# A vision tower's token stage: products read straight from the image tile, joined with the first normalization

## The chip, the cores and the metric

The kernel runs on one core of a Trainium2 chip. The metric is the device time of one execution in microseconds. A core has five engines that work side by side: TensorE (PE; its weight loads are PEld), VectorE (DVE), ScalarE (ACT), GpSimd (POOL) and SyncE (SP), which here only issues DMAs. They meet at semaphores. TensorE writes into eight PSUM banks of 128 partitions x 512 fp32.

## The reference

64 images of 3 x 224 x 224 become tokens, one attention block runs over them, then four experts and a head. The change touches the first two lines only:

```
patches = X.reshape(B, 3, 8, 28, 8, 28).transpose(0, 2, 4, 1, 3, 5).reshape(B, 64, 2352)
tokens  = einsum('bpi,hi->bph', patches, W) + b
tokens  = concat([class_token, tokens], axis=1) * pos_embed        # (64, 65, 128)
h = tokens + attention(layernorm(tokens))
h = h + experts(layernorm(h))
```

So each of the 64 patches of an image is a sum over 3 channels x 28 rows x 28 columns, and the normalization is over the 128 features of a token: subtract the mean, divide by the root of the variance + 1e-5. All of it is in fp32.

## The kernel before

Features lie in partitions and tokens in the free dimension: `h` and `z` are 128 x 4160 (64 images x 65 tokens). The stages follow each other in blocks; every engine finishes a block before the next is opened, and at each opening the semaphores of the stage before are cleared.

**Token stage** (`tokens_stage`, L201). A chunk is four images (`XI`), so there are 16. SP loads a chunk with 12 DMAs (L253), one for each channel and image, into `image[84, slot, 4, 8, 224]`: partition = channel x 28 + row within the patch, and in the free dimension image, patch row and the 224 pixels of a line. There are two slots. The sum over a patch's 28 columns is made as products that add up in PSUM. For one column the moving operand has 84 rows and 256 tokens, and these 256 elements lie 28 elements (112 bytes) apart in `image`. The kernel doesn't multiply them there. It first copies them side by side into `packed[128, slot, 21, 256]`: 21 columns by VectorE (L338), and the rows of the other 7 columns are spread over partitions 96 to 127 of the same 21 places, two parts by ScalarE (L306) and one by VectorE (L340). So 21 products of 128 rows (L292) do the work of 28. VectorE then stores the result with bias and positional factor into `h` (L345, `store`). The order on VectorE is written out: pack of a chunk, then store of the one before. SP loads a slot again when both packers are done with it (L260, L261); TensorE waits for both packers and for the store of two chunks before (L290).

Ahead of the loop the token weights are loaded as `w_rows[128, 84 x 28]`, turned by 28 transposes (L279), whose stationary operand takes 84 elements 28 apart, and copied to `w_cols` (L319, L322). The unused partitions are zeroed by memsets (L268, L311, L312).

**First normalization** (`norm_stage`, L362, called with the tag "n1_"). Ten steps of 416 tokens. For each: TensorE multiplies by `center` (L416, identity minus 1/128), ScalarE copies it out (L440) and squares it (L442), TensorE multiplies by `mean` (L422, 1/128 everywhere), ScalarE takes the root (L434), VectorE the reciprocal (L453), and GpSimd multiplies into `z` (L401). Buffers are double. The same function runs once more behind the attention ("n2_").

**First attention** (`first_attention_stage`) then reads `z`. `shared.ring` is a tile of 128 x 7680 fp32 that only later stages use.

Of the kernel before, what the change touches and what calls it, by code (L numbers as in the profile page):

```python
# [16 lines left out]
ALU = mybir.AluOpType  # L17
ACT = mybir.ActivationFunctionType
AX = mybir.AxisListType
ds = bass.ds  # L20

P = 128
# [175 lines left out]

def tokens_stage(nc, signals, ps, io, h0, ident, w_rows):  # L201

    XI = 4
    SLOTS = 2
    TRIPS = IMAGES // XI // SLOTS
    NP = GRID * GRID
    WHOLE = 21
    SPLIT = ((0, 32), (32, 64), (64, ROWS))
    HIGH = 96
    assert WHOLE == len(SPLIT) * (PATCH - WHOLE)  # L210
    with ExitStack() as ctx:
        sb = lambda name, shape: ctx.enter_context(nc.sbuf_tensor(name, shape, F32))
        sem = signals.stage()
        image = sb("image", [ROWS, SLOTS, XI, GRID, SIDE])
        packed = sb("packed", [P, SLOTS, WHOLE, XI * NP])
        w_cols = sb("w_cols", [P, WHOLE, P])
# [4 lines left out]
        clsp = sb("clsp", [P, 1])  # L221
        loaded = [sem(f"image_loaded{i}") for i in range(SLOTS)]
        consts, w_in = sem("consts_loaded"), sem("w_loaded")
        id_zero, id_done = sem("id_zeroed"), sem("id_done")
        turned, kept, padded = sem("w_turned"), sem("w_kept"), sem("rows_padded")
        packed_act, packed_dve = sem("packed_by_act"), sem("packed_by_dve")
        summed, stored, cls_done = sem("tok_summed"), sem("tok_stored"), sem("cls_done")
        block = open_block(nc, ctx, signals)
        turns = PATCH // 4

        def whole(s):

            return (packed[0:ROWS, s].rearrange("p q (r j) -> p q r j", j=GRID),
                    image[:, s].rearrange("p b g (j q) -> p q (b g) j", q=PATCH)[:, 0:WHOLE])

        def part(s, k):

            lo, hi = SPLIT[k]
            return (packed[HIGH:HIGH + hi - lo, s, k:WHOLE:len(SPLIT)].rearrange("p q (r j) -> p q r j", j=GRID),
                    image[lo:hi, s].rearrange("p b g (j q) -> p q (b g) j", q=PATCH)[:, WHOLE:PATCH])  # L240

        @block.sync
        def _(sp):
            sp.dma_start(w_rows[:, :], io["tok_W"]).then_inc(w_in, 16)
# [4 lines left out]
            def load(chunk, s):  # L249
                for c in range(CHANNELS):  # L250
                    for b in range(XI):
                        src = io["x"][ds(chunk * XI + b, 1), c].rearrange("a (g p) w -> p (a g) w", p=PATCH)
                        sp.dma_start(image[c * PATCH:(c + 1) * PATCH, s, b], src).then_inc(loaded[s], 16)  # L253

            for s in range(SLOTS):
                load(s, s)
            with sp.Fori(0, TRIPS - 1) as i:
                for s in range(SLOTS):

                    sp.wait_ge(packed_act, BASE + i * SLOTS + s + 1)  # L260
                    sp.wait_ge(packed_dve, BASE + i * SLOTS + s + 1)  # L261
                    load((i + 1) * SLOTS + s, s)

        @block.gpsimd
        def _(pool):
            make_identity(pool, ident, id_zero, id_done)
            pool.wait_ge(id_done, BASE + 1)
            pool.memset(packed[64:P, 1], 0.0).then_inc(padded, 1)  # L268

        @block.tensor  # L270
        def _(pe):
            pe.wait_ge(w_in, BASE + 16)
            pe.wait_ge(id_done, BASE + 1)
            w_view = w_rows[:, :].rearrange("p (r q) -> p r q", q=PATCH)
            for g in range(turns):
                if g >= 4:
                    pe.wait_ge(kept, BASE + g - 3)
# [7 lines left out]
            with pe.Fori(0, TRIPS) as i:  # L285
                for s in range(SLOTS):
                    pe.wait_ge(packed_act, BASE + i * SLOTS + s + 1)
                    pe.wait_ge(packed_dve, BASE + i * SLOTS + s + 1)

                    pe.wait_ge(stored, BASE + i * SLOTS + s - 1)  # L290
                    for q in range(WHOLE):
                        m = pe.matmul(ps[:, s, 0:XI * NP], w_cols[:, q, :], packed[:, s, q, :],  # L292
                                      start=(q == 0), stop=(q == WHOLE - 1))
                    m.then_inc(summed, 1)

        @block.scalar
        def _(act):
            act.wait_ge(padded, BASE + 3)
            with act.Fori(0, TRIPS) as i:
                for s in range(SLOTS):  # L300
                    act.wait_ge(loaded[s], BASE + (i + 1) * 16 * CHANNELS * XI)

                    act.wait_ge(summed, BASE + i * SLOTS + s - 1)
                    for k in range(2):
                        to, of = part(s, k)
                        op = act.copy(to, of)  # L306
                    op.then_inc(packed_act, 1)

        @block.vector
        def _(dve):  # L310
            dve.memset(packed[64:P, 0], 0.0).then_inc(padded, 1)  # L311
            dve.memset(w_cols[64:P], 0.0).then_inc(padded, 1)  # L312
            dve.wait_ge(padded, BASE + 3)
            for g in range(turns):
                dve.wait_ge(turned, BASE + g + 1)
                now = ps[0:ROWS, g % 4, :].rearrange("p (j m) -> p j m", j=4)
                here = min(max(WHOLE - 4 * g, 0), 4)
                if here:
                    op = dve.tensor_copy(w_cols[0:ROWS, 4 * g:4 * g + here, :], now[:, 0:here, :])  # L319
                for k, (lo, hi) in enumerate(SPLIT if here < 4 else ()):  # L320
                    at = len(SPLIT) * (4 * g + here - WHOLE) + k
                    op = dve.tensor_copy(w_cols[HIGH:HIGH + hi - lo, at:at + len(SPLIT) * (3 - here) + 1:len(SPLIT), :],  # L322
                                         now[lo:hi, here:4, :])
                op.then_inc(kept, 1)
# [8 lines left out]
            def pack(i, s):  # L333
                dve.wait_ge(loaded[s], BASE + (i + 1) * 16 * CHANNELS * XI)

                dve.wait_ge(summed, BASE + i * SLOTS + s - 1)
                to, of = whole(s)
                dve.tensor_copy(to, of)  # L338
                to, of = part(s, 2)
                dve.tensor_copy(to, of).then_inc(packed_dve, 1)  # L340

            def store(i, s):
                dve.wait_ge(summed, BASE + i * SLOTS + s + 1)
                out = h0[:, ds((i * SLOTS + s) * XI * SEQ, XI * SEQ)].rearrange("p (b s) -> p b s", s=SEQ)
                dve.scalar_tensor_tensor(  # L345
                    out=out[:, :, 1:SEQ], in0=ps[:, s, 0:XI * NP].rearrange("p (b t) -> p b t", t=NP),
                    scalar=bias[:, 0:1], in1=pos[:, 1:SEQ].unsqueeze(1).broadcast_to([P, XI, NP]),
                    op0=ALU.add, op1=ALU.mult).then_inc(stored, 1)

            pack(0, 0)  # L350
            pack(0, 1)
            store(0, 0)
            with dve.Fori(0, TRIPS - 1) as i:
                pack(i + 1, 0)
                store(i, 1)
                pack(i + 1, 1)
                store(i + 1, 0)
            store(TRIPS - 1, 1)

def norm_stage(nc, signals, ps, tag, src, dst, add, spill):  # L362
# [2317 lines left out]
```

## Time and profile before

| | us |
|---|---|
| median of 3 runs | 4192.47 (4190.81 to 4195.63) |
| profiled execution, own time | 4191.02 |
| its span in the trace | 4189.3 |
| TensorE busy over the span | 3695.9 (88%) |
| VectorE busy | 2841.8 (68%) |
| ScalarE busy | 2150.3 (51%) |
| GpSimd busy | 1278.5 (31%) |

The profile is one execution. Matmuls overlap in it (their ends are modelled), so what matters of them is how far apart they start. An fp32 product shows as two records. "Idle before" is the time in which an engine did nothing ahead of a group, with what ended it.

### The profile page before, as it was taken

Reading aid. Unit: us, or ns where it says so; the run is one execution under the profiler, and the core shown is the slowest. Engines: PE = TensorE matmul, PEld = TensorE weight load, DVE = VectorE, ACT = ScalarE, POOL = GpSimd, SP = SyncE. Lnnn points to the kernel's source line nnn. Section 1 sums busy time; section 2 is a strip of 40 time slices with the busy share of each in tenths; the row PEclk is TensorE's granted clock in tenths of the full one; section 3 lists DMA queues with packets and bytes.
Section 4 is the critical chain, followed back from the end, with each engine's and each line's share of the span. In section 5 each row is a group of like instructions: output and inputs, shape, how many; then the busy total and the mean of one; then the engine's idle time right before and its main releaser. Section 6 shows DMA issues by size and latency. Waiting matters only on the chain. (4 is left out here: it accounts for less than half of the span.)

```text
span 4189.3 us, 98294 instructions
## 1 busy us (share of the span) xinstructions
PE 3695.9 (88%) x36068; PEld 2265.2 (54%) x36068; DVE 2841.8 (68%) x5015; ACT 2150.3 (51%) x4378; POOL 1278.5 (31%) x1076
## 2 busy tenths in 40 slices
PE   5869689979988998952999999999999959999998
PEld 4645346646655655631555555555555527666665
DVE  8966568858858857876666666666666664555555
ACT  4536437737746755755444444444444445555554
POOL 0027537627726736744000000000000003444443
PEclk8889899989999999975999999999999978999999
DMA  8910100010010011025111111111111131111111
GB/s 174 176 33 0 52 18 2 1 56 2 0 42 16 0 42 32 0 87 157 46 50 48 45 48 50 48 44 48 49 49 43 49 103 52 54 53 53 53 53 30
DMA packets 392895, 205.07 MB, mean 49 GB/s; under 512 B 151221, under 2 KB 386474, under 8 KB 392106
## 3 DMA queue, kind: packets, MB, share of 16 engines
q1 hardware_dynamic: 392354, 203.09, 18.9%
q8 instruction: 88, 1.44, 0.1%
q14 instruction: 61, 0.50, 0.0%
q10 hardware_dynamic: 392, 0.03, 0.0%
HBM read 145.55 MB, written 57.51 MB: 48 GB/s over the span
## 5 line engine op out<-in xcount | busy, mean ns | idle before, releaser
L1827 PE MATMUL banks<-l_w,l_xs 128*64 128x512 f16 x6240 | 722.3, 381 | 15.0 <-DVE l_xs L1875 14.2
L1827 PE MATMUL banks<-l_w,l_hs 128*64 128x512 f16 x6144 | 705.8, 379 | 1.7 <-DVE l_hs L1881 1.7
L1827 PEld LDWEIGHTS banks<-l_w,l_xs 128*64 128x64 f16 x6240 | 344.6, 110 | 330.7 <-issue 25.6
L1827 PEld LDWEIGHTS banks<-l_w,l_hs 128*64 128x64 f16 x6144 | 348.3, 110 | 316.7 <-DVE l_hs L1881 2.2
L194 POOL MEMSET h_ident<- 128x128 f32 x1 | 0.2, 204 | 1444.3 <-POOLq L81 1444.3
L985 POOL TENSOR_TENSOR ax_p<-ax_p,ax_ri 128x520 f32<-128x520 f32 (+1 forms) x256 | 320.0, 1251 | 267.4 <-DVE ax_ri L1185 267.4
L1932 DVE SCALAR_TENSOR_TENSOR l_gates<-banks,l_unscale,l_bias 128x1024 f32<-128x1024 f32 x260 | 333.8, 1284 | 96.1 <-PE banks L1827 94.7
L1988 ACT ACTIVATE l_gates<-l_gates 128x768 f32<-128x768 f32 x260 | 219.1, 843 | 347.4 <-DVE l_gates L1932 347.4
L2259 PE MATMUL banks<-h_mem,h_w 128*128 128x320 f16 x2496 | 357.9, 300 | 1.0 <-DMA h_mem<-mem_scratch 1.0
L2554 ACT ACTIVATE h_work<-banks,h_bias,h_factor 128x320 f32<-128x320 f32 x312 | 192.3, 616 | 262.8 <-PE banks L2259 259.1
L2259 PEld LDWEIGHTS banks<-h_mem,h_w 128*128 128x128 f16 x2496 | 244.4, 98 | 94.9 <-issue 1.6
L956 POOL TENSOR_TENSOR ax_km<-ax_k,ax_mask 128x512 f32<-128x512 f32 x256 | 290.6, 1136 | 6.0 <-PE banks L1067 6.0
L1992 ACT ACTIVATE l_ig<-l_cell 128x256 f32<-128x256 f32 x260 | 108.3, 416 | 358.2 <-DVE l_cell L1949 356.2
L1263 ACT ACTIVATE ax_p<-ax_p 128x520 f32<-128x520 f32 (+1 forms) x256 | 170.5, 666 | 202.7 <-DVE ax_p L1177 202.0
L999 PE MATMUL banks<-ax_x,w_in 128*128 128x256 f16 (+1 forms) x1632 | 198.3, 274 | 81.3 <-DVE ax_x L1149 54.1
L1945 DVE TENSOR_TENSOR l_ig<-l_gates 128x256 f32<-128x256 f32 x256 | 109.0, 426 | 210.0 <-ACT l_gates L1989 210.0
L1172 DVE TENSOR_REDUCE ax_mx<-banks 128x8 f32<-128x520 f32 (+1 forms) x256 | 186.0, 727 | 84.0 <-PE banks L1067 83.8
L292 PE MATMUL banks<-packed,w_cols 128*128 128x256 f32 x672 | 174.8, 427 | 56.8 <-DVE packed L340 56.8
L999 PEld LDWEIGHTS banks<-ax_x,w_in 128*128 128x128 f16 x1632 | 146.6, 100 | 122.4 <-DVE ax_x L1149 68.8
L1177 DVE TENSOR_TENSOR ax_p<-banks,ax_mx 128x520 f32<-128x520 f32 (+1 forms) x256 | 187.9, 734 | 31.2 <-DVE ax_mx L1172 13.9
L1953 DVE TENSOR_TENSOR l_hid<-l_gates,l_ig 128x256 f32<-128x256 f32 x260 | 110.8, 426 | 130.1 <-ACT l_ig L1992 130.1
L292 PEld LDWEIGHTS banks<-packed,w_cols 128*128 128x128 f32 x672 | 144.4, 217 | 86.9 <-issue 62.9
(306 smaller groups left out, 7180.4 us busy)
## 6 DMA issues: line engine op xcount, KB each, us to landing
image<-in_x_dram SPq DMA_DIRECT2D x192, 196.0 KB
l_x<-x_scratch SPq DMA_DIRECT2D x130, 256.0 KB, 3.0
mem_scratch<-l_hs SPq DMA_DIRECT2D x520, 64.0 KB, 1.9
h_mem<-mem_scratch SPq DMA_DIRECT2D x104, 320.0 KB, 3.7
x_scratch<-x_out SPq DMA_DIRECT2D x4, 4160.0 KB, 16.4
raw_in<-in_L_ffn_attn_in_w_dram SPq DMA_DIRECT2D x4, 768.0 KB, 4.5
h_scratch<-x_out SPq DMA_DIRECT2D x1, 2080.0 KB, 6.5
z_scratch<-z SPq DMA_DIRECT2D x1, 2080.0 KB, 11.6
```

Of the source, the lines that this page charges most:

```text
L292: m = pe.matmul(ps[:, s, 0:XI * NP], w_cols[:, q, :], packed[:, s, q, :], start=(q == 0), stop=(q == WHOLE - 1))
L956: pool.tensor_tensor(self.km[:, s % 2], self.k[:, par, :, s, :].unsqueeze(2).broadcast_to([P, KD, 4, self.KEYS]), self.mask4[:, :].unsquee ...
L985: pool.tensor_tensor(self.p[:, v, :, 0:k], self.p[:, v, :, 0:k], self.ri[:, v, :, 0:k].unsqueeze(3).broadcast_to([P, 2, k, SEQ]), ALU.mult ...
L999: mm = pe.matmul(bank, w_in[:, k, b, at:at + P], x[:, a, k], start=(k == 0 and i == 0), stop=(k == KD - 1 and i == len(PASSES) - 1))
L1172: dve.tensor_reduce(self.mx[:, s % 2, :, 0:k], now, AX.X, ALU.max).then_inc(self.maxed, 1)
L1177: dve.tensor_tensor(self.p[:, v, :, 0:k], now, self.mx[:, s % 2, :, 0:k].unsqueeze(3).broadcast_to([P, 2, k, SEQ]), ALU.subtract).then_inc ...
L1263: act.activation(self.p[:, s % 4, :, 0:k], self.p[:, s % 4, :, 0:k], ACT.Exp, scale=SCALE).then_inc(self.exped, 1)
L1827: mm = pe.matmul(ps[d * HALF:(d + 1) * HALF, 2 * z + n, :], lhsT, w_of[e][:, d, kk, b, n * 512:(n + 1) * 512], start=(kk == 0 and turn_ == ...
L1932: dve.scalar_tensor_tensor(out=gz.rearrange("p (n c) -> p n c", n=2), in0=ps[:, 2 * z:2 * z + 2, :], scalar=unscale[:, e:e + 1], in1=bias[ ...
L1988: act.activation(gates[:, z, 0:3 * D], gates[:, z, 0:3 * D], ACT.Sigmoid).then_inc(gated, 1)
L2259: mm = pe.matmul(ps[:, bank, 0:W], w[:, e, b, here:here + P], moving(k, a), start=(k == 0 and turn_ == 0), stop=(k == nk - 1 and turn_ == 2))
L2554: act.activation(dst[:, m, :], ps[:, bank, 0:W], func, bias=bias(m), scale=factor[:, e, at:at + 1]).then_inc(S[name + "_kept"], 1)
```

## The change

The token stage and the first normalization become one stage. Nothing is copied: the moving operand of each product is the image tile itself, 84 rows and 256 elements 112 bytes apart (`column`), so there are 28 products for a chunk instead of 21. The packing, its tiles and the memsets are gone. There are four image slots; the fourth lies in `shared.ring`. SP loads a slot again when its products are done (`summed`). The loops of the stage are written out. The normalization goes in steps of one chunk (260 tokens), with its products behind those of the next chunks on TensorE and its reciprocals behind the stores on VectorE. The second normalization is as before.

```
 # SP
+            for n in range(CHUNKS):
+                s = n % SLOTS
+                if n >= SLOTS:
+                    sp.wait_ge(summed, BASE + n - SLOTS + 1)
                 for c in range(CHANNELS):
                     for b in range(XI):
+                        src = io["x"][n * XI + b, c].rearrange("(g p) w -> p g w", p=PATCH)
+                        sp.dma_start(image[s][c * PATCH:(c + 1) * PATCH, b], src).then_inc(loaded[s], 16)
 # GpSimd
+            for n in range(CHUNKS):
+                pool.wait_ge(inverted, BASE + n + 1)
+                pool.tensor_tensor(span(z, n), xc[:, n % 2, :], rs[:, n % 2, :], ALU.mult).then_inc(normed, 1)
 # TensorE
+            for n in range(CHUNKS + 2):
+                if n < CHUNKS:
+                    pe.wait_ge(loaded[n % SLOTS], BASE + (n // SLOTS + 1) * 16 * CHANNELS * XI)
+                    if n >= 2:
+                        pe.wait_ge(stored, BASE + n - 1)
+                    for q in range(PATCH):
+                        m = pe.matmul(ps[:, n % 2, 0:XI * NP], w_cols[:, q, :], column(n % SLOTS, q),
+                                      start=(q == 0), stop=(q == PATCH - 1))
                     m.then_inc(summed, 1)
+                if 1 <= n <= CHUNKS:
+                    pe.wait_ge(stored, BASE + n)
+                    if n >= 3:
+                        pe.wait_ge(copied, BASE + n - 2)
+                    pe.matmul(ps[:, 2 + (n - 1) % 2, 0:SPAN], center[:, :], span(h0, n - 1), start=True,
+                              stop=True).then_inc(centered, 1)
+                if n >= 2:
+                    pe.wait_ge(squared, BASE + n - 1)
+                    if n >= 4:
+                        pe.wait_ge(rooted, BASE + n - 3)
+                    pe.matmul(ps[:, 4 + n % 2, 0:SPAN], mean[:, :], sq[:, n % 2, :], start=True, stop=True).then_inc(varied, 1)
 # ScalarE
+            for n in range(CHUNKS + 3):
+                if 2 <= n < CHUNKS + 2:
+                    m = n - 2
+                    act.wait_ge(centered, BASE + m + 1)
+                    if m >= 2:
+                        act.wait_ge(normed, BASE + m - 1)
+                    act.copy(xc[:, m % 2, :], ps[:, 2 + m % 2, 0:SPAN]).then_inc(copied, 1)
...
+                    act.activation(sq[:, m % 2, :], xc[:, m % 2, :], ACT.Square).then_inc(squared, 1)
+                if n >= 3:
+                    m = n - 3
+                    act.wait_ge(varied, BASE + m + 1)
...
+                    act.activation(sd[:, m % 2, :], ps[:, 4 + m % 2, 0:SPAN], ACT.Sqrt, bias=eps[:, 0:1]).then_inc(rooted, 1)
 # VectorE
+            for n in range(CHUNKS + 4):
+                if 1 <= n <= CHUNKS:
+                    m = n - 1
+                    dve.wait_ge(summed, BASE + m + 1)
+                    dve.scalar_tensor_tensor(
...
+                if n >= 4:
+                    m = n - 4
+                    dve.wait_ge(rooted, BASE + m + 1)
+                    if m >= 2:
+                        dve.wait_ge(normed, BASE + m - 1)
+                    dve.reciprocal(rs[:, m % 2, :], sd[:, m % 2, :]).then_inc(inverted, 1)
 # front
-        tokens_stage(nc, signals, ps, io, h, ident, z[:, 0:ROWS * PATCH])
+        tokens_stage(nc, signals, shared, ps, io, h, z, ident)
         attended = sb("attended", [P, TOKENS])
-        norm_stage(nc, signals, ps, "n1_", h, z, None, None)
```

## Rows read from the trace of the kernel before

**Rows 1.** The page: span, and the DMA engines' busy share in 40 slices.
```profile
span 4189.3 us, 98294 instructions
DMA  8910100010010011025111111111111131111111
```

**Rows 2.** Stretches: start:end us, length, each engine busy (records), clock, DMA share, GB/s.
```profile
35.30:228.40 193.10, 153.13 (x590) 126.52 (x589) 175.25 (x42) 106.74 (x36) 0.00 (x0) 0.87 0.92 175
228.40:250.55 22.15, 20.63 (x83) 17.06 (x81) 13.01 (x4) 6.94 (x2) 0.00 (x0) 0.88 0.00 0
250.55:292.60 42.05, 19.18 (x40) 7.40 (x40) 27.53 (x11) 17.79 (x31) 11.28 (x14) 0.87 0.00 0
```

**Rows 3.** Groups by line and form, 0 to 450 us: busy us, mean ns | idle before.
```profile
L292 PE MATMUL banks<-packed,w_cols 128*128 128x256 f32 x672 | 174.8, 427 | 56.8 <-DVE packed L340 56.8
L338 DVE COPY packed<-image 84x5376 f32<-84x5376 f32 x16 | 160.5, 10034 | 21.4 <-DMA image<-in_x_dram 21.4
L306 ACT COPY packed<-image 32x1792 f32<-32x1792 f32 x32 | 111.6, 3486 | 42.2 <-DMA image<-in_x_dram 42.0
L340 DVE COPY packed<-image 20x1792 f32<-20x1792 f32 x16 | 31.9, 1995 | 0.2
```

**Rows 4.** Timeline at the end of the token stage: start us, length us, instruction.
```profile
227.33 12.37 PE L292 MATMUL banks<-packed,w_cols 128*128 128x256 f32 x42 [3.17 <-DVE packed L340]
...
228.41 10.03 DVE L338 COPY packed<-image 84x5376 f32<-84x5376 f32 x1 [0.81 <-DMA image<-in_x_dram]
...
240.70 9.33 PE L292 MATMUL banks<-packed,w_cols 128*128 128x256 f32 x42 [1.00 <-DVE packed L340]
250.07 0.48 DVE L345 SCALAR_TENSOR_TENSOR x_out<-banks,tok_bias,pos 128x256 f32<-128x256 f32 x1 [9.09 <-PE banks L292]
```

**Rows 5.** Timeline of the first two chunks.
```profile
22.13 9.93 DVE L338 COPY packed<-image 84x5376 f32<-84x5376 f32 x1 [2.94 <-DMA image<-in_x_dram]
...
34.31 11.61 PE L292 MATMUL banks<-packed,w_cols 128*128 128x256 f32 x42 [15.83 <-DVE packed L340]
35.27 10.04 DVE L338 COPY packed<-image 84x5376 f32<-84x5376 f32 x1 [1.21 <-DMA image<-in_x_dram]
```

**Rows 6.** Stretches early in the token stage.
```profile
20.00:30.00 10.00, 0.00 (x0) 0.00 (x0) 7.87 (x1) 7.78 (x3) 0.00 (x0) 0.50 1.00 180
...
40.00:60.00 20.00, 15.24 (x70) 12.78 (x68) 17.98 (x5) 10.60 (x4) 0.00 (x0) 0.99 0.98 181
```

**Rows 7.** First normalization: two groups, then the timeline at its end.
```profile
L453 DVE RECIPROCAL n_rs<-n_sd 128x416 f32<-128x416 f32 x10 | 27.5, 2752 | 13.3 <-ACT n_sd L434 11.8 <-POOL z L401 1.4
...
L442 ACT ACTIVATE n_sq<-n_xc 128x416 f32<-128x416 f32 x10 | 5.5, 549 | 0.3
...
291.49 1.06 POOL L401 TENSOR_TENSOR z<-n_xc,n_rs 128x416 f32<-128x416 f32 x1 [2.64 <-DVE n_rs L453]
294.18 0.42 SPq L1293 DMA_DIRECT2D a_rows<-in_L_attn_w_qkv_dram  x1
```

**Rows 8.** Groups of 260 columns in the attention stage.
```profile
L602 PE MATMUL banks<-a_x,a_cols 128*128 128x260 f32 x64 | 19.2, 425 | 1.0 <-DVE a_cols L1314 1.0
L784 ACT COPY a_k<-banks 128x260 f32<-128x260 f32 x16 | 6.0, 376 | 1.0 <-PE banks L602 0.4
L571 POOL TENSOR_TENSOR a_p<-a_p,a_ri 128x260 f32<-128x260 f32 x48 | 30.7, 640 | 29.0 <-DVE a_ri L739 29.0
```

**Rows 9.** Strided and contiguous fp32 reads; weight loads (min/median/max or mean ns).
```profile
L2612 ACT COPY h_z2s<-h_h 128x4160 f32<-128x4160 f32 x1 | 7.6, 7640 | 0.0
L1988 ACT ACTIVATE l_gates<-l_gates 128x768 f32<-128x768 f32 x260 | 219.1, 843 | 347.4 <-DVE l_gates L1932 347.4
L279 PEld LDWEIGHTS banks<-ident,z x7: 152/154/178, 12.4 to 13.2; 128*84 128x84 f32 x7
L691 PEld LDWEIGHTS banks<-ident,a_p x256: 133/137/138, 309.4 to 461.7; 128*65 128x65 f32 x128
L699 PEld LDWEIGHTS banks<-a_pt,a_v 65*32 65x32 f32 x896 | 15.3, 109 | 9.6 <-issue 9.6
```

More of the change, by code:

```diff
@@ L213, in tokens_stage @@
         sem = signals.stage()
-        image = sb("image", [ROWS, SLOTS, XI, GRID, SIDE])
-        packed = sb("packed", [P, SLOTS, WHOLE, XI * NP])
-        w_cols = sb("w_cols", [P, WHOLE, P])
+        w_rows = z[:, 0:ROWS * PATCH]
+        own = sb("image", [ROWS, SLOTS - 1, XI, GRID, SIDE])
+        image = [own[:, s] for s in range(SLOTS - 1)]
+        image.append(shared.ring[0:ROWS, 0:XI * GRID * SIDE].rearrange("p (b g w) -> p b g w", b=XI, g=GRID))
+        w_cols = sb("w_cols", [ROWS, PATCH, P])
         pos_rows = sb("pos_rows", [SEQ, P])
@@ L221, in tokens_stage, with column @@
         clsp = sb("clsp", [P, 1])
+        center = sb("n1_center", [P, P])
+        mean = sb("n1_mean", [P, P])
+        eps = sb("n1_eps", [P, 1])
+        xc = sb("n1_xc", [P, 2, SPAN])
+        sq = sb("n1_sq", [P, 2, SPAN])
+        sd = sb("n1_sd", [P, 2, SPAN])
+        rs = sb("n1_rs", [P, 2, SPAN])
         loaded = [sem(f"image_loaded{i}") for i in range(SLOTS)]
         consts, w_in = sem("consts_loaded"), sem("w_loaded")
-        id_zero, id_done = sem("id_zeroed"), sem("id_done")
-        turned, kept, padded = sem("w_turned"), sem("w_kept"), sem("rows_padded")
-        packed_act, packed_dve = sem("packed_by_act"), sem("packed_by_dve")
+        id_zero, id_done, zero, ready = sem("id_zeroed"), sem("id_done"), sem("n1_zero"), sem("n1_ready")
+        turned, kept = sem("w_turned"), sem("w_kept")
         summed, stored, cls_done = sem("tok_summed"), sem("tok_stored"), sem("cls_done")
+        centered, copied, squared, varied, rooted, inverted, normed = [
+            sem("n1_" + n) for n in ("centered", "copied", "squared", "varied", "rooted", "inverted", "normed")]
         block = open_block(nc, ctx, signals)
         turns = PATCH // 4
[L231 to L240, printed above, removed]
+        def column(s, q):
+            return image[s].rearrange("p b g (j q) -> p q (b g) j", q=PATCH)[:, q]
+        span = lambda a, n: a[:, n * SPAN:(n + 1) * SPAN]
         @block.sync
         def _(sp):
-            sp.dma_start(w_rows[:, :], io["tok_W"]).then_inc(w_in, 16)
+            sp.dma_start(w_rows, io["tok_W"]).then_inc(w_in, 16)
             sp.dma_start(pos_rows[:, :], io["pos"]).then_inc(consts, 16)
@@ L247, in _ @@
             sp.dma_start(cls[:, :], io["cls"].rearrange("a p -> p a")).then_inc(consts, 16)
-            def load(chunk, s):
+            for n in range(CHUNKS):
+                s = n % SLOTS
+                if n >= SLOTS:
+                    sp.wait_ge(summed, BASE + n - SLOTS + 1)
                 for c in range(CHANNELS):
                     for b in range(XI):
[L252 to L262, printed above, removed]
+                        src = io["x"][n * XI + b, c].rearrange("(g p) w -> p g w", p=PATCH)
+                        sp.dma_start(image[s][c * PATCH:(c + 1) * PATCH, b], src).then_inc(loaded[s], 16)
         @block.gpsimd
@@ L284, in _ @@
             pe.wait_ge(kept, BASE + turns + 1)
[L285 to L293, printed above, removed]
-                    m.then_inc(summed, 1)
+            pe.wait_ge(ready, BASE + 3)
@@ L296, in _ @@
         @block.scalar
         def _(act):
[L298 to L307, printed above, removed]
+            act.wait_ge(ready, BASE + 3)
@@ L309, in _ @@
         @block.vector
         def _(dve):
-            dve.memset(packed[64:P, 0], 0.0).then_inc(padded, 1)
-            dve.memset(w_cols[64:P], 0.0).then_inc(padded, 1)
-            dve.wait_ge(padded, BASE + 3)
             for g in range(turns):
                 dve.wait_ge(turned, BASE + g + 1)
[L316 to L324, printed above, removed]
+                dve.tensor_copy(w_cols[:, 4 * g:4 * g + 4, :],
+                                ps[0:ROWS, g % 4, :].rearrange("p (j m) -> p j m", j=4)).then_inc(kept, 1)
@@ L331, in _ @@
             dve.tensor_copy(h0_view[:, :, 0], clsp[:, :].broadcast_to([P, IMAGES])).then_inc(cls_done, 1)
[L333 to L358, printed above, removed]
+            dve.wait_ge(cls_done, BASE + 2)
+            for n in range(CHUNKS + 4):
[3 more added lines that the diff above has]
+                    dve.scalar_tensor_tensor(
+                        out=h0_view[:, m * XI:(m + 1) * XI, 1:SEQ],
+                        in0=ps[:, m % 2, 0:XI * NP].rearrange("p (b t) -> p b t", t=NP), scalar=bias[:, 0:1],
+                        in1=pos[:, 1:SEQ].unsqueeze(1).broadcast_to([P, XI, NP]), op0=ALU.add, op1=ALU.mult).then_inc(stored, 1)
+                if n >= 4:
+                    m = n - 4
+                    dve.wait_ge(rooted, BASE + m + 1)
+                    if m >= 2:
+                        dve.wait_ge(normed, BASE + m - 1)
+                    dve.reciprocal(rs[:, m % 2, :], sd[:, m % 2, :]).then_inc(inverted, 1)
 def norm_stage(nc, signals, ps, tag, src, dst, add, spill):
```

25 lines of the change are left out of this document (16 added, 9 removed).

## The prediction

> **What bounds the kernel now.** The page shows a span of 4189.3 us and, in its slices, the DMA engines near full only in the first 6% [rows 1]. That is the stage the change rewrites, so I cut the start of the trace into stretches [rows 2]. Until 228.4 us the image streams in with a DMA share of 0.92 while VectorE is busy 175 of 193 us and TensorE 153; from there to 250.55 the last chunk is packed and multiplied with no DMA at all; from 250.55 to 292.6 the first normalization runs alone, every engine below two thirds busy. Everything behind 292.6 is unchanged text, so the change is worth what it takes off these 292.6 us.
>
> In the token stage a chunk of four images costs VectorE 10.03 + 1.99 us of packing plus 0.48 for the store, and ScalarE two copies of 3.49 [rows 3, 4]. A slot is loaded again only when it is packed, so load and packing alternate on two slots: chunk 0 is there at 22.1 us, chunk 15 at 228.4, 13.75 us a chunk. With a full queue the loads take less: chunk 1 landed 13.1 us after chunk 0 [rows 5], and the fullest windows move 180 to 181 GB/s [rows 6], which is 13.35 us for the 2.408 MB of a chunk. So DMA is the floor of this stage, and the packing adds 0.4 us a chunk and 12 us at the end, where chunk 15 is packed with nothing beside it.
>
> **Part 1: packing goes.** 12.0 us of VectorE and 7.0 of ScalarE a chunk disappear. Beside the DMA they hid, apart from the 0.4 us a chunk (6 us over 15 chunks) and 12.3 us between landing (228.4) and first product (240.7) of the last chunk [rows 4].
>
> **Part 2: products, 28 for 21.** The last run of 42 records (two to a product) took 9.33 us at full clock, 0.218 us a record after the first [rows 4]. 56 records are 12.2 us. The first run after an idle stretch costs more: 11.61 us where the stretch before had a granted clock of 0.50, the lower level (1.2 GHz), and 12.37 for a later one with gaps [rows 5, 4], so 2.3 to 3.0 us once, at the start. Then TensorE also gets the two normalization products of 260 columns, four records of 0.222 us, 0.9 us a chunk (the 260-column rows of the attention stage have the same length as the 256-column ones, within the per-column step [rows 8]). Sum: 13.1 us a chunk against 13.35 for DMA. The two are almost level, so TensorE has gaps of a few tenths of a microsecond, where now they are 1 to 5 us, and I expect it to stay at full clock.
>
> The moving operand is what no row shows: 256 fp32 elements 112 bytes apart instead of side by side. Bounds come from the nearest rows of strided fp32 reads [rows 9, 3]. ScalarE read 4160 elements 260 bytes apart in 7.64 us, 1.84 ns each, while its contiguous 768 took 0.843 us, 1.1 ns with the fixed part: about a doubling. VectorE's 20-partition copy reads this very image with this very step at 1.11 ns. TensorE's own weight loads read the token weights with this same 112-byte step: 84 columns in 154 ns, where 32 and 65 contiguous columns took 109 and 137 ns, 0.85 ns a column; that line gives 153 ns for 84. No stall is left to put down to the step. I take this row, because it is the same engine and fp32 too, and a moving record of 0.218 us is 0.85 ns a column, the same pace. So the term is 12.2 us; the ends kept for the range are 0.85 and 1.84 ns a column.
>
> The Trainium skill speaks against it. "SBUF — State Buffer", Specifications (TRN2), gives 16-byte cachelines that need at least two hits per line for full bandwidth. With one fp32 element per line that would double each record, and the sum would be the slow rival's below; ScalarE's row agrees with it, the weight loads' does not.
>
> **Part 3: loads run free.** Four slots, and a slot is given back by the products instead of the packing. The load of chunk n waits for the products of n-4, which end three chunk times before the queue needs it, so SP never lets the queue run dry. The weights go ahead of chunk 0 as now, so chunk 0 is ready at 22.1. Chunk 15 lands at 22.1 + 15 x 13.35 = 222.3. TensorE alone would begin it at 22.1 + 2.6 + 15 x 13.1 = 221.2. The later one decides: products end at 222.3 + 12.2 + about 0.5 for waits = 235.0. The loops that are now written out add instruction fetches; no row before shows TensorE on long written-out text beside full queues, so I take nothing for them, as the loads of chunk n are covered by the products of the chunks before, and keep 1 us a chunk as the upper end (16 us, the high end of the forecast's own range).
>
> **Part 4: normalization moves beside the products.** Removed: all 42.0 us of the stage [rows 2]. Added per chunk, scaled from 416 to 260 columns or read at 260: reciprocal 2.75 x 260/416 = 1.72 us on VectorE, multiply 0.64 on GpSimd, copy 0.38, square about 0.4 and root about 0.45 on ScalarE [rows 7, 8]. VectorE then does 0.5 + 1.7 us in 13.35, ScalarE 1.2, GpSimd 0.64: all hidden under DMA. The added waits on TensorE stand in its queue ahead of the next products: "stored" of the chunk before, "copied" and "squared" of the one before that. All three are signalled at the latest 5 us after the products before, thus 8 us early.
>
> What doesn't hide is the tail, because the order is laid out with a lag. On VectorE the reciprocal of chunk n-4 stands behind the store of n-1, so when the last products end, four reciprocals (12 to 15) are still to come, and the copy of a chunk waits for the multiply of the one two before it. Followed through, from the products' end: store 0.5, reciprocal 12 to 2.2, multiply 3.0, copy and square of 14 to 3.9, root 13 to 4.3, reciprocal 13 to 6.1, multiply 6.8, copy and square of 15 to 7.7, root 14 to 8.2, reciprocal 14 to 9.9, reciprocal 15 to 11.7, multiply to 12.4. The stage ends at 235.0 + 12.4 = 247.4, where now the last multiply ends at 292.55 [rows 7]: 45.1 us less. One opening of a block between stages goes with it and is inside those 42 us; the attention's opening clears 22 semaphores instead of 10, for which I give back 0.3 us. Its first transfer follows now 1.6 us behind the last multiply [rows 7], and will again.
>
> **Sum.** 4191.02 (the profiled execution; 1.7 outside its span) - 44.8 = 4146.2. The median of the runs is 1.45 above the profiled one, so 4147.7 us.
>
> **Rivals.**
> Slow rival, slower than before: the moving read pays for the step as ScalarE does. A doubled record is 0.436 us, a chunk 24.4 + 0.9 = 25.3 us, TensorE becomes the bound: 22.1 + 16 x 25.3 + 11.5 = 438.4, 145.9 us later than 292.5, time 4338. At ScalarE's 1.84 ns (0.471 us a record) it is 4371. It decides from the point where TensorE's chunk is (292.5 - 22.1 - 11.5)/16 = 16.2 us, thus 0.273 us a record, 1.07 ns a column. For it: ScalarE's row, and the 84-partition copy at 10.03 us for 5376 elements, 1.87 ns. Against it: the weight loads, and the 20-partition copy. Half-way stands VectorE's 1.11 ns: 0.284 us a record, 16.8 us a chunk, 302 us, time 4202.
> Second rival, a smaller gain: TensorE falls to the lower clock between chunks, as it does now in gaps of 2 to 5 us (mean clock 0.87 [rows 2]). 2 us more a chunk make TensorE the bound at 15.1 us: 22.1 + 241.6 + 11.5 = 275, time 4175. Against it: the gaps become short.
> Third, that the change gains only its packing half: if a wait chain held the normalization behind the products, TensorE would stall 3 to 4 us a chunk for it, 16.5 us a chunk, no gain: 4195. The program order above gives each signal a chunk of time, so little speaks for this.
>
> **How the numbers follow.** Forecast 0.66, with a range of its own of 4140 to 4160 (the low end has DMA at 13.1 us a chunk, the high end 1 us more a chunk on TensorE). Smaller gain 0.07, half-way 0.06, slow rival 0.18, third 0.03. What a measurement can tell from no change is 0.2%, 8.4 us. Faster: forecast and second rival, 0.72 with a share of the half-way case below its centre. Same: 0.04. Slower: 0.24. To leave out no more than 2 in 10 the range must reach the doubled record: 4139 to 4340.
>
> **What would show it.** A record of the products at 378 to 382 ns and 56 of them in about 12.4 us: part 2 right; records twice as far apart and a DMA share near 0.5: the slow rival. DMA share at 0.98 or more until 222 us: part 3. TensorE's granted clock at 1.00 from 40 us on: no second rival. Last multiply some 12 us behind the last product, with four reciprocals between: part 4. The attention's first transfer at about 249.3 us. The forecast is wrong if TensorE's chunk exceeds 14 us.

## The result and the profile after: slower by 4.4%

The changed kernel takes 4375.51 us (median of 4 runs, 4371.53 to 4377.8), the kernel before 4191.67 beside it (4 runs, 4190.81 to 4195.63). The ratio is 1.0436, 95% interval 1.0418 to 1.0454. The forecast of 4147.7 is wrong, and so is its range of 4139 to 4340; what came is the slow rival at ScalarE's price, 4371. The profiled execution took 4376.95 us.

The page after, against [rows 1]: its span, and 40 slices with the granted clock (tenths of full) and the DMA share.

```profile
span 4375.2 us, 98154 instructions
...
PEclk5555798999999999997699999999999997999999
DMA  7442001001001001002511111111111123121111
```

The loads, which filled the first 6% of the span before, now spread over four slices at falling shares, and the clock stands at its lower level (0.50, 1.2 GHz) for as long. The stretches of the stage, against [rows 2]:

```profile
22.10:50.00 27.90, 27.54 (x59) 18.55 (x60) 0.48 (x1) 0.00 (x0) 0.00 (x0) 0.50 1.00 184
50.00:200.00 150.00, 150.00 (x324) 98.76 (x323) 7.47 (x8) 8.11 (x16) 2.20 (x3) 0.53 0.57 109
200.00:430.00 230.00, 230.00 (x497) 150.43 (x496) 17.35 (x16) 9.28 (x24) 5.88 (x8) 0.54 0.33 63
```

TensorE is busy 150 us of 150 and 230 of 230 while DMA falls to 0.57 and 0.33 and VectorE does 7.5 us of work in 150: TensorE alone sets the pace. The groups, against [rows 3] (the packing lines are gone; L297 are the products, L360 the normalization's reciprocals, L273 its multiplies):

```profile
L297 PE MATMUL banks<-image,w_cols 84*128 84x256 f32 x672 | 315.7, 647 | 8.3 <-DMA image<-in_x_dram 8.3
...
L360 DVE RECIPROCAL n_rs<-n_sd 128x260 f32<-128x260 f32 x16 | 28.2, 1767 | 4.3 <-ACT n_sd L331 4.2
...
L273 POOL TENSOR_TENSOR z<-n_xc,n_rs 128x260 f32<-128x260 f32 x16 | 11.7, 734 | 460.4 <-DVE n_rs L360 460.4
```

647 ns is a record's duration; its pace is read from how far apart records start. The weight loads, one to a record, in a stretch where the clock was full, and the clock of two windows, one in it and one behind it:

```profile
161.10 0.21 PEld L297 LDWEIGHTS banks<-image,w_cols 84*128 84x128 f32 x1 [0.19 <-issue]
161.56 0.21 PEld L297 LDWEIGHTS banks<-image,w_cols 84*128 84x128 f32 x1 [0.26 <-issue]
162.03 0.21 PEld L297 LDWEIGHTS banks<-image,w_cols 84*128 84x128 f32 x1 [0.26 <-issue]
162.50 0.21 PEld L297 LDWEIGHTS banks<-image,w_cols 84*128 84x128 f32 x1 [0.26 <-issue]
```

```profile
161.00:162.00 1.00, 1.00 (x3) 0.42 (x2) 0.00 (x0) 0.96 (x3) 0.00 (x0) 1.00 0.95 178
...
170.00:174.00 4.00, 4.00 (x10) 2.76 (x9) 0.00 (x0) 0.00 (x0) 0.00 (x0) 0.50 0.34 61
```

They start 0.467 us apart at a granted clock of 1.00, and the ones from 170.43 on, at 0.50, stand 0.467 apart too (170.43, 170.90, 171.36). So the clock does not set the pace. That the read does is what the first experiment shows; by it an element costs 0.467/256 = 1.82 ns. 56 records take 26.1 us where 12.2 were forecast. With 0.9 to 1.7 us of normalization a chunk is 27.6 us: products run from 22.46 to 463.8.

The end of the stage, where the forecast had put four reciprocals:

```profile
464.29 1.78 DVE L360 RECIPROCAL n_rs<-n_sd 128x260 f32<-128x260 f32 x1
...
468.19 1.78 DVE L360 RECIPROCAL n_rs<-n_sd 128x260 f32<-128x260 f32 x1 [2.12 <-ACT n_sd L331]
...
472.09 3.42 DVE L360 RECIPROCAL n_rs<-n_sd 128x260 f32<-128x260 f32 x2 [2.12 <-ACT n_sd L331]
...
475.59 0.73 POOL L273 TENSOR_TENSOR z<-n_xc,n_rs 128x260 f32<-128x260 f32 x1 [0.91 <-DVE n_rs L360]
478.18 0.41 SPq L1294 DMA_DIRECT2D a_rows<-in_L_attn_w_qkv_dram  x1
```

The last multiply ends at 476.32, where before it ended at 292.55 [rows 7]: 183.8 us later. The profiled executions are 185.9 us apart, the medians 183.8.

### The profile page after: what moved, and what is told of

Its sections match the earlier page's. It is cut to its first block and busy times, and to the rows that moved or that the text cites. A ratio compares the mean times of both kernels' runs of the same rounds, so it can differ in the third digit from the quotient of the medians.

```text
span 4375.2 us, 98154 instructions
## 1 busy us (share of the span) xinstructions
PE 3951.9 (90%) x36316; PEld 2407.2 (55%) x36316; DVE 2636.4 (60%) x4982; ACT 2031.9 (46%) x4357; POOL 1275.0 (29%) x1081
## 5 line engine op out<-in xcount | busy, mean ns | idle before, releaser
L297 PE MATMUL banks<-image,w_cols 84*128 84x256 f32 x672 | 315.7, 647 | 8.3 <-DMA image<-in_x_dram 8.3
L297 PEld LDWEIGHTS banks<-image,w_cols 84*128 84x128 f32 x672 | 204.2, 304 | 116.3 <-issue 113.2
L1173 DVE TENSOR_REDUCE ax_mx<-banks 128x8 f32<-128x520 f32 (+1 forms) x256 | 185.9, 726 | 88.3 <-PE banks L1068 88.0
L1178 DVE TENSOR_TENSOR ax_p<-banks,ax_mx 128x520 f32<-128x520 f32 (+1 forms) x256 | 187.9, 734 | 29.8 <-DVE ax_mx L1173 12.4
```

The costliest lines, as they stand in the source:

```text
L297: m = pe.matmul(ps[:, n % 2, 0:XI * NP], w_cols[:, q, :], column(n % SLOTS, q), start=(q == 0), stop=(q == PATCH - 1))
L1173: dve.tensor_reduce(self.mx[:, s % 2, :, 0:k], now, AX.X, ALU.max).then_inc(self.maxed, 1)
L1178: dve.tensor_tensor(self.p[:, v, :, 0:k], now, self.mx[:, s % 2, :, 0:k].unsqueeze(3).broadcast_to([P, 2, k, SEQ]), ALU.subtract).then_inc ...
```

## Experiments

A run that was timed in rounds has an interval; the others are one profiled execution with its time. Line numbers differ a little between the kernels. Unless said otherwise the edit is made in the changed kernel.

### Moving elements side by side

Each product reads 256 neighbouring elements of the image tile, so the output isn't the tokens; all else is equal.

```
-            return image[s].rearrange("p b g (j q) -> p q (b g) j", q=PATCH)[:, q]
+            flat = image[s].rearrange("p b g w -> p (b g w)")
+            at = q // 1 * 1 * XI * NP + q % 1
+            return flat[:, at:at + 1 * (XI * NP - 1) + 1:1]
```

> The changed kernel, but the 256 elements of each product's moving operand lie side by side in the image tile instead of 112 bytes apart (the tile is read as if it were packed, so the tokens are not the reference's). Same 28 products, same 84 rows, same waits. Theory A (TensorE's moving read pays for the step; the low granted clock follows from it): records 0.218 us apart instead of 0.467, granted clock near 1.00, DMA share near 1 until about 222 us, time about 4148. Rival B (the low clock is the cause, because of 84 rows or of written-out text, and the step costs little): records 0.43 us apart at a granted clock of 0.50, time about 4340. If both count, records stay above 0.25 us and the time lands between 4180 and 4330.

4175.22 us (5 runs), ratio to before 0.9962 (0.9948 to 0.9976). 200 us come back, so the step is the cause. The timeline shows that 28 more are missing:

```profile
71.20 24.10 PE L299 MATMUL banks<-image,w_cols 84*128 84x256 f32 x56
95.09 1.07 PE L306 MATMUL banks<-x_out,n_center 128*128 128x260 f32 x2
95.96 0.71 PE L312 MATMUL banks<-n_sq,n_mean 128*128 128x260 f32 x2
96.51 12.25 PE L299 MATMUL banks<-ring,w_cols 84*128 84x256 f32 x56
```

```profile
22.50:95.00 72.50, 72.50 (x170) 57.33 (x171) 0.97 (x2) 2.08 (x3) 0.00 (x0) 0.50 0.89 162
...
98.00:200.00 102.00, 102.00 (x473) 89.64 (x472) 15.61 (x16) 8.95 (x23) 5.14 (x7) 1.00 0.99 175
```

Three chunks run at the lower clock, 24.1 us each, though TensorE is busy 72.5 us of 72.5. The clock rises only behind the first four records in a row of 128 rows, the two normalization products from 95.09 on; then a chunk takes 12.25, as forecast. The expectation of about 4148 had not seen these three chunks.

### Steps of 8 and of 16 bytes

The same with every second and every fourth element (`flat[:, at:at + 511:2]`, `flat[:, at:at + 1021:4]`).

> As the side-by-side kernel, but the moving elements lie 8 bytes apart (two fp32 in each 16 bytes). Theory A with 16-byte lines, as the Trainium skill's page SBUF — State Buffer, Specifications (TRN2), has them: two reads fall into a line, so full pace, records 0.218 us apart and about 4148. Rival A2 (any step beyond the next element costs the same): records 0.467 us apart and about 4375. Between them, a cost that grows with the step: about 0.24 us.

> As the side-by-side kernel, but the moving elements lie 16 bytes apart (one fp32 in each 16 bytes). Theory A with 16-byte lines: every read opens a new line, so records 0.467 us apart as at 112 bytes and about 4375. If the line is longer than 16 bytes (32 or 64): 0.218 us and about 4148.

4183.11 and 4364.26 us (4148 and 4375 expected; the 8-byte kernel too has three chunks of 24.1 us at the lower clock). First a chunk with 8 bytes at a granted clock of 1.00, then one with 16 at 0.50:

```profile
110.47 12.86 PE L299 MATMUL banks<-image,w_cols 84*128 84x256 f32 x56
```

```profile
128.31 25.57 PE L299 MATMUL banks<-image,w_cols 84*128 84x256 f32 x56
```

A record (the chunk less the last record's own 0.388 or 0.632 us, over 55) takes 0.2268 and 0.4534 us. 256 elements 8 bytes apart touch 128 pieces of 16 bytes, 16 bytes apart 256: 1.77 ns a piece in both. The 16-byte kernel also had a stretch at 1.00: its weight loads start at 183.21, 183.66, 184.11 and 184.56 us, 0.45 apart, so this price does not follow the clock. Side by side the elements touch 64 pieces, which would be 0.113 us and hides under the 0.2155 us that 256 columns take anyway at full clock. There a record takes the longer of columns x 0.84 ns and pieces x 1.77 ns; at 112 bytes a piece is 1.82. At the lower clock the columns take twice as long, 0.43 us a record, which hides 8 bytes altogether (24.1 us a chunk with it and without it) and 16 bytes nearly.

### bfloat16 halves, same step

```
+            flat = image[s].rearrange("p b g w -> p (b g w)").bitcast(BF16)
+            return flat[:, 2 * q + 1:2 * q + 1 + 2 * PATCH * (XI * NP - 1) + 1:2 * PATCH]
```

The products take the upper halves of weights and pixels as bf16 numbers: one record to a product instead of two, the same 256 places.

> The changed kernel, with each product on the upper halves of the fp32 values read as bf16, so with one record instead of two, the moving elements still 112 bytes apart (tokens only bf16-exact). Theory A1 (each address costs TensorE's moving read about 1.7 to 1.8 ns, whatever the type and the number of passes over it): 256 addresses, 0.43 to 0.47 us a record, 28 records a chunk = 12.0 to 13.1 us, so DMA bounds and the time is about 4150 to 4160. Rival A3 (an fp32 record reads its elements twice, so an address costs half of that): 0.22 to 0.24 us a record, 6.5 us a chunk. Both leave the time near 4145 to 4160; the distance of the records decides.

```profile
79.19 13.24 PE L299 MATMUL banks<-image,w_cols 84*128 84x256 bf16 x28
```

4162.85 us. 28 records in 13.24 us, less the last one's 0.647, are 0.466 us each, the fp32 record's pace. So neither the bytes of an element nor its type count, only how many places are read. Half the records halve the bill, and the granted clock stayed at 0.50 (22.5 to 200 us) beside a DMA share of 1.00.

### Weights strided, moving operand side by side

Beside the edit of the first experiment the stationary operand takes every 28th element of `w_cols`.

> The side-by-side kernel, but now the stationary operand is read with the step: its 128 fp32 elements lie 112 bytes apart in w_cols (tokens not the reference's). Theory G (weight loads do not pay for the step, as the token weights' turning in the kernel before seemed to show: 84 columns in 154 ns): records 0.2155 us apart at full clock, time as the side-by-side kernel's, about 4175. Rival H (the weight read pays as the moving read does, and what hid it in the kernel before is that a transpose's load is shorter than the spacing of its records): 128 addresses at 1.7 to 1.8 ns are 0.22 us a load or, if an fp32 load reads twice, 0.44 us, records 0.45 us apart, time about 4360.

```profile
124.63 12.88 PE L300 MATMUL banks<-image,w_cols 84*128 84x256 f32 x56
```

4181.32 us; 0.227 us a record against 0.2155. 128 places at 1.77 ns are 0.227: the weight load sets the pace and pays the same price. Side by side such a load takes 0.112 us at full clock (next section), so the step doubles it as well. It barely shows, because the product's 256 columns take 0.2155 anyway.

### The weight loads by themselves

Four groups of 28 instructions ahead of chunk 0, back to back.

```
+ pe.transpose(ps[0:ROWS, 7, 0:P], w_view[:, :, k], ident[:, :])
+ pe.transpose(ps[0:ROWS, 7, 0:P], w_rows[:, 84 * k:84 * k + 84], ident[:, :])
+ pe.matmul(ps[0:ROWS, 7, 0:32], w_view[:, :, k], ident[:, 0:32], start=True, stop=True)
+ pe.matmul(ps[0:ROWS, 7, 0:32], w_rows[:, 84 * k:84 * k + 84], ident[:, 0:32], start=True, stop=True)
```

> The changed kernel with four extra groups of 28 instructions on TensorE ahead of chunk 0, each back to back: transposes whose stationary operand is 84 columns of the token weights 112 bytes apart (as the kernel's own are), the same with the 84 columns side by side, and then fp32 products of 32 moving columns with the same two stationary operands, where the load is longer than the product and sets the pace. What is open is why the prediction's row (84 strided columns in 154 ns) showed no price for the step. Theory 1: the duration in that row is no measure of the read (154 ns is also 84 times 1.83 ns), and the strided load costs 1.77 ns an address as the moving operand does; then the strided product loads stand about 150 ns apart for a load, and the ones side by side clearly closer. Theory 2: a fp32 load is so slow by itself that the step hides under it (the 128 column load of the kernel with strided weights stood at 0.227 us against 0.213); then the two groups of products stand within 10% of each other and the row could not have shown the step whatever its price. The transposes, whose pace the 128 moving columns set (0.16 us apart in the kernel before), should be alike by either. The whole time is of no interest: 4376 plus about 2 us.

The groups in this order, strided, side by side, strided, side by side:

```profile
14.12 3.07 PEld L288 LDWEIGHTS banks<-ident,z 128*84 128x84 f32 x28 [1.49 <-DVE w_cols L345]
17.14 3.07 PEld L290 LDWEIGHTS banks<-ident,z 128*84 128x84 f32 x28
20.20 8.51 PEld L292 LDWEIGHTS banks<-ident,z 128*84 128x84 f32 x56
28.61 7.94 PEld L294 LDWEIGHTS banks<-ident,z 128*84 128x84 f32 x56
```

The transposes stand 0.11 us apart either way. Of the product loads, two to a product, the strided ones stand 0.150 apart and those side by side 0.140, within the 10% of theory 2. But the two groups didn't run at one clock. The stretches, and two groups of the changed kernel's own trace, further on, whose products have a single moving column and 128 weight columns side by side:

```profile
20.40:24.80 4.40, 4.40 (x32) 4.40 (x31) 0.00 (x0) 0.00 (x0) 0.00 (x0) 1.00 1.01 188
28.70:36.20 7.50, 7.50 (x55) 7.50 (x56) 0.00 (x0) 0.00 (x0) 0.00 (x0) 0.50 0.99 187
```

```profile
707.83 5.26 PE L1463 MATMUL banks<-x_vec,raw_in 128*128 128x1 f32 x24
1707.40 2.26 PE L1463 MATMUL banks<-x_vec,raw_in 128*128 128x1 f32 x19
```

The clock fell at 25.0 us, within the strided group, and its loads stand 0.150 apart before and behind: 84 places at 1.77 ns are 0.149. The group side by side had 0.50 throughout. The two lines of the changed kernel give 0.213 us a load at 0.50 and 0.112 at 1.00, thus 1.67 and 0.87 ns a column. At 0.50 that makes 0.140 for 84 columns, what the group took; at 1.00 it would be 0.073 (an estimate, by columns), and the strided load takes twice that. So theory 1 holds: the load of a product pays for the step, and the lower clock hid it here. The forecast's row [rows 9] was one of transposes, whose loads show no price at all. Why they go at 0.110 us with the step, below 84 x 1.77 = 0.149, stays open. The whole took 4391.19 us, 13 more than expected: the groups lie ahead of chunk 0, whose products began at 37.17 instead of 22.46, and TensorE had nothing to spare.

### Side by side, with the clock kept up

The first experiment, and 20 products over 128 rows (40 records of 256 columns) while chunk 0 is still in flight. In the first experiment the clock was at 1.00 from 10.8 us on, behind the transposes of the weights, and fell at 17.7, as TensorE waited for the first image; here it stays at 1.00 from 12.2 us on. So the extra products hold the clock rather than lift it.

```
+            for k in range(20):
+                at = k % 9 * XI * NP
+                pe.matmul(ps[:, 7, 0:XI * NP], center[:, :], z[:, at:at + XI * NP], start=True, stop=True)
```

> The side-by-side kernel (tokens not the reference's) with 20 products of 128 rows x 256 columns put on TensorE ahead of chunk 0, where it waits for the first image; their result is not used. Theory E (what kept the side-by-side kernel at the 1.2 GHz level for its first three chunks, 24.1 us each instead of 12.25, is that products of 84 rows do not raise the granted clock, but keep it once it is up; the 128-row products of the normalization raised it at 96 us): the clock is 1.00 from the first chunk, products at 0.2155 us a record throughout, last products end at about 235 us, time about 4148. Rival F (something of the stage's first 70 us, such as DMA traffic or the written-out text's first pass, holds the clock down): three slow chunks again, time about 4175.

```profile
36.00:200.00 164.00, 160.20 (x727) 137.13 (x728) 23.14 (x23) 15.10 (x34) 7.04 (x10) 1.00 1.00 180
```

4146.95 us (4 runs, 4143.44 to 4148.8), ratio 0.989 (0.9873 to 0.9906). That is the forecast's 4147.7: with the step and the low clock gone, DMA is full at 1.00, chunks take 12.25 to 12.35 us and the last products end at 236.4 (235.0 forecast). The clock is worth 4175.22 - 4146.95 = 28 us.

### The changed kernel, with the clock kept up

The same 20 products ahead of the changed kernel's own reads.

> The changed kernel as it is, with 20 products over 128 rows ahead of chunk 0 and nothing else. Theory: the address step of the moving operand sets 0.467 us a record at either clock, and a granted clock that is lifted first falls again within some us though TensorE stays busy; the time is about 4375 (4372 to 4380). Rival: the low granted clock is a cause of the slow records, and once lifted stays up as in the side-by-side kernel; then the chunks take less than 26 us and the time lies anywhere from 4150 to 4340.

```profile
23.00:26.00 3.00, 3.00 (x9) 1.54 (x8) 0.00 (x0) 0.00 (x0) 0.00 (x0) 1.00 0.99 176
26.00:28.00 2.00, 2.00 (x5) 0.83 (x4) 0.00 (x0) 0.00 (x0) 0.00 (x0) 1.00 1.01 176
28.00:30.00 2.00, 2.00 (x6) 1.33 (x5) 0.00 (x0) 0.00 (x0) 0.00 (x0) 0.53 0.99 177
30.00:34.00 4.00, 4.00 (x10) 2.68 (x9) 0.00 (x0) 0.00 (x0) 0.00 (x0) 0.50 0.99 184
```

4374.67 us, no gain. The clock stood at 1.00 at the start of the products and fell within 5 us with TensorE busy throughout. The low clock follows from the slow reads and is not their cause.

### Packing on VectorE alone

From the changed kernel: two image and two packed slots, and VectorE copies all 28 columns side by side; ScalarE copies nothing in the packing. The 28 products and the joined normalization stay.

```
+ dve.tensor_copy(packed[n % 2].rearrange("p q (r j) -> p q r j", j=GRID),
+                 image[n % SLOTS].rearrange("p b g (j q) -> p q (b g) j", q=PATCH)).then_inc(packed_dve, 1)
```

> All of the reference. One stage with the normalization, as in the changed kernel, but VectorE copies each chunk side by side (one copy of 84 x 7168, all 28 columns, nothing on ScalarE), two image slots and two packed slots, 28 products from the packed tile. Theory C (VectorE was slowed to 1.87 ns an element in the kernel before only by ScalarE reading the same partitions; alone it takes the 1.08 ns of its 20-partition copy): the copy takes 7.8 us, VectorE is busy 10.1 us a chunk, DMA stays the bound, the stage ends at about 222.3 + 7.8 + 12.2 + 13 = 255 us and the time is about 4154. Rival D (84 partitions at this step cost 1.87 ns whatever ScalarE does): 13.4 us a copy, VectorE 15.7 us a chunk, the stage ends at about 298 us, time about 4197.

```profile
L353 DVE COPY packed<-image 84x7168 f32<-84x7168 f32 x8 | 54.9, 6858 | 15.8 <-DMA image<-in_x_dram 15.8
...
L274 POOL TENSOR_TENSOR z<-n_xc,n_rs 128x260 f32<-128x260 f32 x16 | 44.1, 2754 | 238.3 <-DVE n_rs L367 238.3
```

4184.24 us (10 runs), ratio 0.9989 (0.9977 to 1.0001): no change that can be told. But the copy reads the same image with the same step at 6858/7168 = 0.96 ns an element, where before, beside ScalarE's packing, it took 10034/5376 = 1.87 [rows 3]. VectorE's packing fell from 12.0 to 6.9 us a chunk, though it now copies all columns. That ScalarE's reads had slowed it is the likely cause and not shown: no run has the old copy without ScalarE. The run again lost three chunks to the lower clock.

The 2754 ns of GpSimd's multiply are a mean of two cases, five of 7.1 to 7.2 us and eleven of 0.73. One of each:

```profile
119.16 6.77 DVE L353 COPY ring<-image 84x7168 f32<-84x7168 f32 x1
119.40 7.14 POOL L274 TENSOR_TENSOR z<-n_xc,n_rs 128x260 f32<-128x260 f32 x1 [115.21 <-DVE n_rs L367]
...
184.16 0.73 POOL L274 TENSOR_TENSOR z<-n_xc,n_rs 128x260 f32<-128x260 f32 x1 [5.75 <-DVE n_rs L367]
184.34 7.29 DVE L353 COPY packed<-image 84x7168 f32<-84x7168 f32 x1 [0.26 <-DMA image<-in_x_dram]
```

A multiply that begins behind VectorE's copy ends 0.6 us after it; where the multiply came first, the copy took 7.29 us instead of 6.77. The second of the two waits for the first.

### Packing on VectorE, with the clock up, three ways

First with 36 extra products as above.

> All of the reference. The kernel that packs with VectorE alone, with 36 products of 128 rows ahead of chunk 0 whose result is not used. Theory E: clock 1.00 from the first chunk, chunk 0's products begin at about 29.5 us, 13.0 us a chunk on TensorE against 13.35 to 14.1 us for the loads on two slots, last copy ends at about 229 to 238 us, last products at 242 to 251, stage end at 254 to 263 us: time 4153 to 4162. Rival F: as without the extra products, 4184.

4154.65 us (4 runs), ratio 0.9902 (0.9885 to 0.9918). Then without extra products: the packed tile and the weights get 128 rows, 84 to 127 zero, and each of the 28 products takes all 128.

```
-        beside = sb("packed", [ROWS, PATCH, XI * NP])
+        beside = sb("packed", [P, PATCH, XI * NP])
-        w_cols = sb("w_cols", [ROWS, PATCH, P])
+        w_cols = sb("w_cols", [P, PATCH, P])
```

> The kernel that packs on VectorE alone, but its 28 products a chunk take 128 rows of the packed tile (rows 84 to 127 hold zeros) in place of 84, and nothing else warms TensorE. First theory: what lifts the granted clock is how many rows a product takes, whatever their content. Then the clock is at 1.00 within a few us of the first product, there are no chunks of 24.1 us, and the time is about 4156 (4184.2 less two and a third slow chunks' excess of 12 us each). Rival: rows of zeros lift nothing; then the first three chunks take 24.1 us again and the time is about 4184.

```profile
33.81 14.23 PE L299 MATMUL banks<-packed,w_cols 128*128 128x256 f32 x56 [7.63 <-DVE packed L358]
47.88 12.25 PE L299 MATMUL banks<-ring,w_cols 128*128 128x256 f32 x56
```

4154.21 us (4 runs), ratio 0.991 (0.9895 to 0.9925). One chunk takes 2 us more, and no chunk 24.1: its records stand 0.43 us apart until 37.4 us, 3.5 us after the first, and 0.216 from 37.7 on. With 128 rows the pace of the full clock comes though 44 of them are zeros. At last the copy in two halves, a shorter normalization chain and 28 extra products.

```
+                        if q % HALF == 0:
+                            pe.wait_ge(packed_dve, BASE + 2 * n + 1 + q // HALF)
-            for n in range(CHUNKS + 4):
+            for n in range(CHUNKS + 3):
```

> The packing kernel with 28 warming products, the copy of a chunk in two halves of columns so that the products wait for a half only, and a shorter chain in the normalization (the reciprocal runs three tiles behind and not four, the root stands ahead of the copy and the square on ScalarE). If the tail and the wait for the first copy are on the path, as the traces of the changed kernel (12.6 us from last product to the end) and of the packing kernel show, 3.4 us go for the half copy and about 3.7 in the tail: about 4147.5 against 4154.65 for the warmed packing kernel. Rival: transfers set the pace of the middle chunks (DMA share 1.00 there), and what is gained at the start is waited for later; then only the tail's gain stays, about 4151.

```profile
186.22 0.60 PE L316 MATMUL banks<-n_sq,n_mean 128*128 128x260 f32 x2
189.00 23.94 PE L303 MATMUL banks<-packed,w_cols 84*128 84x256 f32 x56 [2.18 <-DVE packed L360]
...
214.46 13.32 PE L303 MATMUL banks<-ring,w_cols 84*128 84x256 f32 x56
```

4148.36 us (5 runs, 4139.97 to 4160.17), ratio 0.9893 (0.9878 to 0.9909). The median stands where expected (4147.5), but the interval doesn't part it from the two others. The profiled execution, 4160.17, shows one source of its spread: behind a wait of 2.18 us for a copy the clock fell, and the 84-row products ran a whole chunk at half pace; it rose again behind the next four records of 128 rows. That lost 12 us. All three take about 1% less than the kernel before.

## Why the prediction was wrong

**What bounds the kernel, and DMA as the floor** held: 4146.95 us with a DMA share of 1.00 once nothing else was slow.

**Part 2 failed, at the moving operand.** The step took its price from the weight loads, "No stall is left to put down to the step. I take this row, because it is the same engine and fp32 too". Measured: 1.82 ns a column, not 0.85, 0.467 us a record, 26.1 us a chunk, and TensorE became the bound. Two things were wrong with the row. They were loads of transposes, which show no price for the step (0.110 us apart with it and without it); the same columns loaded for a product cost 0.150, twice what side by side would. And durations were compared, three of them put on a line, where the pace of a row of records was needed. The ends kept for the read's price (0.85 and 1.84 ns) did hold the truth; the choice between them was the error. The full price was worked out as 4371 and left outside the range of 4139 to 4340, which reached only the doubled record at 4338. The stage ended 5.9 us later than the rival had it: 27.57 us a chunk instead of 27.3 (4.3 in 16), a tail of 12.6 instead of 11.5, and a start 0.4 later.

The rule of "SBUF — State Buffer", Specifications (TRN2) in the Trainium skill, at least two hits in each 16-byte line for full bandwidth, was told and given too little weight. The runs agree with it in the main: at full clock two hits a line cost 5%, one hit doubles the record.

**Part 2 also mis-sized the start.** "2.3 to 3.0 us once, at the start" came from products of 128 rows [rows 5]. With 84 rows the clock did not rise in 72.5 us; that cost 28 us in the side-by-side kernel. Without the step the change as written takes 4175, by chance the second rival's time, whose mechanism (gaps between chunks) it is not.

**Part 3** could not show in the changed kernel, where TensorE was late. In the side-by-side kernel with the clock up it was right to 1.4 us, and so was taking nothing for the written-out loops: the chunks there take 12.25 to 12.35 us.

**Part 4 was right.** From last product to last multiply 12.6 us (12.4 forecast), with four reciprocals of 1.77 us (1.72) and the chain in the order followed through. The attention's first transfer came 1.86 us behind it (1.6).

**Slow rival.** It was given 0.18. Its signs all came: records twice as far apart, a DMA share near 0.5. Its price was ScalarE's 1.84 ns; TensorE's is 1.82.

**Third rival.** Its 16.5 us a chunk give 22.1 + 264 + 11.5 = 297.6 us and thus 4198, not the 4195 that stands there. Nothing hangs on it.

## What to carry to other kernels

A product's operand with no more than one element in each 16 bytes cost about 1.8 ns an element here, in fp32 at either clock and in bf16 at the lower. A copy that packs it on VectorE took 0.96 ns an element once and hid beside the loads; even so the joined stage gained only 1%, and only with the clock up. Take the price of an access pattern from a row in which that read sets the pace, measure pace by how far apart records start, and compare two rows only at the same granted clock: at 0.50 the step of the weight loads seemed to cost 7%, at 1.00 it doubles them. Where the cheapest row and a row that doubles it are both at hand and unexplained, the range must reach the dear one in full.

## What the runs showed of the hardware

- TensorE's reads in products: 1.77 ns for each 16-byte piece touched (8- and 16-byte steps), 1.82 at 112 bytes for the moving operand, in fp32 and bf16; 1.77 to 1.79 for the stationary one in fp32. The fp32 reads of 16 and 112 bytes kept their pace at a granted clock of 0.50 and 1.00; the bf16 one was seen at 0.50 alone. Transposes' loads took 1.3 ns a place with the step, which stays open.
- An fp32 load of neighbouring weight columns: 0.87 ns a column at 1.00, 1.67 at 0.50.
- Products over 84 rows did not lift the clock in 72.5 us of unbroken work but kept it at 1.00 once it was up; with 128 rows, 44 of them zeros, the pace of the full clock came within 3.9 us. Strided 84-row products let it fall within 5 us, though TensorE was busy. Four records of 128 rows between chunks lifted it at 95 us in the side-by-side kernel, but not once in 177 us of the bfloat16 kernel and only behind some chunks of the changed one. What decides between these cases is not shown.
- VectorE's strided copy took 1.87 ns an element while ScalarE packed from the same tile and 0.96 without it; the partner was not varied alone. GpSimd's multiply and VectorE's copy exclude each other: whichever starts second waits, up to 6.5 us.
